# Later, larger handling of the probabilities and norms by token in a two-layer cross-attention kernel

## What is computed

```python
# layer 0: rope on q and k, a distance bias on the scores, a gated output
scores = einsum('bhqd,bhkd->bhqk', q, k) * SCALE + temporal_bias
attended = einsum('bhqk,bhkd->bhqd', softmax(scores), v) @ Wout.T + b_out
gate = sigmoid(attended @ Wgate.T + b_gate)
x = x + gate * attended + (1 - gate) * layernorm(x)
x = x + tanh(layernorm(x) @ weight @ aux_weight1 @ aux_weight2 + bias)
# layer 1: attention without a bias (the mask is all ones here), then 8 experts, 2 per token
x = x + attention(layernorm(x) @ wq.T + bq, ctx, mask) @ wo.T + bo
p = softmax(max(layernorm(x) @ gate_W + gate_b, 1e-4))
x = x + sum over the top two experts of comb * (layernorm(x) @ expert_W + expert_b) / 2
```

## Time and profile before

| | us |
|---|---|
| median of 3 runs | 582.25 |
| lowest and highest of them | 575.12, 584.12 |
| the profiled execution, device time | 577.29 |
| its span in the trace | 575.9 |
| PE, ACT, DVE, POOL busy | 514.1, 431.5, 276.9, 171.5 |

### The profile page before, as it was taken

One profiled execution on the slowest core, in us unless ns is written; L12 is line 12 of the kernel. 1 busy time (PEld: TensorE's weight loads), 2 busy tenths in 40 slices (PEclk: granted clock), 3 DMA queues, 4 the chain that ended last, 5 costly groups with the idle time before them and its releaser, 6 DMA issues.

```text
span 575.9 us, 15324 instructions
## 1 busy us (share of the span) xinstructions
PE 514.1 (89%) x6330; PEld 257.7 (45%) x6330; DVE 276.9 (48%) x715; ACT 431.5 (75%) x493; POOL 171.5 (30%) x207
## 2 busy tenths in 40 slices
PE   7688898997979998899999999999999999999993
PEld 4344445444435554455455444434443444344341
DVE  4838555864585255752521342235263435254145
ACT  1257576786678786787879988898979888988841
POOL 4467727584586316750010001000001000000003
PEclk9889999999999999999999999999999999999996
DMA  8497965399258513582364474129213911100000
GB/s 287 102 311 200 290 210 144 117 276 309 64 172 262 194 43 89 176 259 62 81 126 136 116 159 110 31 74 204 78 40 89 218 48 39 32 1 2 10 1 16
DMA packets 51584, 74.53 MB, mean 129 GB/s; under 512 B 11146, under 2 KB 40050, under 8 KB 51506
## 3 DMA queue, kind: packets, MB, share of 16 engines
q1 hardware_dynamic: 40690, 37.92, 26.4%
q0 software_dynamic: 5632, 24.07, 12.3%
q10 hardware_dynamic: 5184, 11.48, 6.3%
HBM read 39.95 MB, written 18.83 MB: 102 GB/s over the span
## 4 chain that ended last, share of the span: by engine, by line
PE 54%; ACT 16%; issue 9%; DVE 9%; POOL 6%; DMA 4%; SPq 1%; ACTq 0%; DVEq 0%; POOLq 0%
PE ps L505 21%; ACT probs L1132 14%; PE ps L481 14%; DMA q_side<-in_far_q 4%; PE ps L416 3%; PE ps L406 2%; PE ps L591 2%; DVE k_swapped L1430 2%; PE ps L410 1%; PE ps L517 1%; ACT k_parts L1159 1%; PE ps L665 1%; PE ps L541 1%; POOL k L977 1%; POOL k L979 1%
## 5 line engine op out<-in xcount | busy, mean ns | idle before, releaser
L1132 ACT ACTIVATE probs<-ps 124x1024 f32<-124x1024 f32 (+1 forms) x416 | 398.6, 1024 | 78.5 <-PE ps L486 51.2
L505 PE MATMUL ps<-probs,values 124*9 124x256 f32 (+1 forms) x3328 | 218.6, 380 | 0.1
L481 PE MATMUL ps<-q_side,k_side 64*124 64x256 bf16 (+1 forms) x1664 | 163.2, 290 | 37.2 <-ACT probs L1132 29.9
L481 PEld LDWEIGHTS ps<-q_side,k_side 64*124 64x124 bf16 (+1 forms) x1664 | 79.3, 130 | 139.9 <-ACT probs L1132 99.9
L505 PEld LDWEIGHTS ps<-probs,values 124*9 124x9 f32 (+1 forms) x3328 | 70.7, 90 | 87.0 <-issue 27.8
L1003 POOL TENSOR_TENSOR post_rstd<-post_rstd,power 128x2 f32<-128x2 f32 x12 | 8.4, 702 | 153.5 <-DVE post_rstd L1627 93.7
L949 POOL DMA_DIRECT2D mask_q<-in_mask x16 | 9.1, 570 | 131.2 <-DVE checks L1489 112.1
L486 PE MATMUL ps<-bias_near,bias_w 64*124 64x84 bf16 (+1 forms) x416 | 42.6, 200 | 0.0
L1430 DVE SCALAR_TENSOR_TENSOR k_swapped<-ps,beta_products,k_table_sb 32x496 f32<-32x496 f32 (+2 forms) x64 | 40.4, 632 | 0.9
L1499 DVE TENSOR_REDUCE sample_max<-ps 128x8 f32<-128x512 f32 x32 | 20.5, 685 | 34.9 <-PE ps L439 34.9
L416 PE MATMUL ps<-w_centred,ctx_turned 128*124 128x256 f32 (+1 forms) x104 | 31.2, 424 | 3.0 <-DVE k_swapped L1430 1.3
(11 more groups left out here) (234 smaller groups left out, 517.7 us busy)
## 6 DMA issues: line engine op xcount, KB each, us to landing
k_side<-k_scratch SPq DMA_DIRECT2D x24, 400.2 KB, 8.6
k_side<-k_parts SPq DMA_DIRECT2D x48, 124.0 KB, 2.4
k_scratch<-k_parts POOLq DMA_DIRECT2D x16, 372.0 KB, 5.2
q_side<-q_parts SPq DMA_DIRECT2D x63, 64.0 KB, 2.4
v_scratch<-values POOLq DMA_DIRECT2D x4, 936.0 KB, 10.7
values<-v_scratch SPq DMA_DIRECT2D x4, 936.0 KB, 13.8
v_scratch<-v POOLq DMA_DIRECT2D x12, 288.0 KB, 5.5
mask_q<-in_mask POOLq DMA_DIRECT2D x8, 400.5 KB, 3.4
```

What stands on the lines that cost most here:

```text
L481: last = pe.matmul(ps[0:width, bank, SQ * i:SQ * (i + 1)], kst[rows, j % 2, 2 * g + i, at], qst[rows, query_slot(j, run), 2 * g + i, :], s ...
L505: last = pe.matmul(ps[32 * i:32 * i + VC, ACC + g // 2, SQ * (g % 2):SQ * (g % 2) + SQ], v[0:rows, j % 2, t, h, :], p[0:rows, u % 4, SQ * ...
L1132: act.activation(p[0:rows, u % 4, :], ps[0:rows, s:s + 2, :].rearrange("p a n -> p (a n)"), ACT.Exp)\
```

## The change

- **From j = 3 on** (`WIDE_FROM`) the probabilities have seven buffers: the four, and three in the context's tiles, which nobody reads any more then. `values` is no longer called twice per visit but `values_at(j, pair)` times, 0 to 3, by tables; the calls of a batch add up to 52, and at most three units are behind. Where a side step runs, few values are called, in other visits three.
- **Other places for side steps.** The gate has five steps instead of nine, at slots 38, 40, 43, 45, 48 (j = 1, 2) or 8, 14, 18, 22, 26 (j = 3, 4). The experts' matmuls, two per step before, stand alone at slots 34, 38, 42, 46, and `weigh` on DVE is cut in two; samples come earlier (j = 4: 30, 34, 38; j > 4: 26, 30, 34) or later (j = 3: 34, 38, 42). Centring the experts' weights is cut in two at slots 42 and 46. `pick` comes one slot earlier. The gate's second tanh stands behind exp(slot + 3) of the third step, the experts' exponent behind exp(slot + 5).
- **Norms by token.** `post_tokens` turns x to tokens on partitions with the identity and at once multiplies the raw x with weights that `fold_weights(2)` has centred once, in j = 1; DVE takes the statistics with `bn_stats` and `bn_aggr` (`post_norm`) and multiplies the spread power into the product. The tanh reads the product from SBUF.
- **Two transfers later.** `load_token_rows(3)` stands behind exp 15 instead of 8 of j = 1; POOL's first `look_at_mask` comes after the keys of chunk 0 of j = 2's keys instead of before.
- **DVE's and SP's order.** At j = 2 `rotate_keys` stands between the two copies of the query parts. From j = 3 on one look at the mask stands ahead of the gate or experts and one ahead of `sample_maxima`. SP's `load_shift` stands ahead of `store_output`.

```diff
 def sample_at(j):
-    return (35, 37, 39) if j == 0 else (33, 35, 37) if j < NB - 1 else (34, 37, 40)
+    if j < NB - 1:
+        return (33, 35, 37) if j else (35, 37, 39)
+    return (34, 38, 42) if j == NB - 1 else (30, 34, 38) if j == NB else (26, 30, 34)
 SPREAD_X_AT = ((0, 14), (0, 17))
 QUERIES_AT = ((0, 15), (0, 18))
 TURN_RSTD_AT = {(0, 22): 1, (1, 6): 2, (2, 6): 3}
 CENTRE_X_AT = ((0, 20), (0, 34))
-FOLD_AT = ((1, 8), (1, 9))
-PICK_AT = 3
+FOLD_AT = ((1, 7), (1, 8), (1, 9))
+WIDE_FROM = NB - 1
+VALUES_AT = {NB - 1: (2, 0, 3, 3, 0, 3, 3, 0, 3, 1, 3, 0, 3, 1, 3, 3, 3, 1, 3, 1, 3, 2, 2, 2, 2, 2),
+             NB: (2, 0, 3, 3, 0, 3, 3, 0, 3, 1, 3, 0, 3, 1, 3, 2, 3, 2, 3, 2, 2, 0, 3, 1, 3, 3)}
+def values_at(j, pair):
+    if j < WIDE_FROM:
+        return 2
+    return VALUES_AT.get(j, (2, 0, 3, 3, 1, 0, 3, 3, 3, 2, 2, 1, 3, 1, 3, 1, 3, 0, 3, 1, 3, 1, 3, 1, 3, 3))[pair]
...
-    base = 38 if j < NB - 1 else 8
-    steps = (0, 2, 3, 5, 6, 8, 9, 11, 12)
-    return steps.index(slot - base) if slot - base in steps else None
-CENTRE_EXPERTS_AT = (NB, 24)
+    steps = (38, 40, 43, 45, 48) if j < NB - 1 else (8, 14, 18, 22, 26)
+    return steps.index(slot) if slot in steps else None
+CENTRE_EXPERTS_AT = ((NB, 42), (NB, 46))
...
-    steps = (8, 10, 22, 24, 26, 29)
+    steps = (8, 10, 20, 22, 34, 38, 42, 46)
...
+        def prob_slot(u):
+            return u % 4 if u < WIDE_FROM * UB else (u - WIDE_FROM * UB) % 7
+        def probs_of(u):
+            slot = prob_slot(u)
+            return p[:, slot, :] if slot < 4 else (ct[:], cn[:], tok[:].rearrange("p t d -> p (t d)"))[slot - 4][:, 0:HG * SQ]
+        def taken_ahead(u):
+            return max((w + 1 for w in range(max(u - 8, 0), u) if prob_slot(w) == prob_slot(u)), default=0)
...
+                    pe.matmul(ps[:, LOW, 0:128], centre[:], w_123[:], start=True, stop=True)
+                    pe.matmul(ps[:, LOW, 128:256], centre[:], late["L1_wq"][:], start=True, stop=True).then_inc(made[LOW], 1)
...
+            def post_tokens(b, k, weights_in, what):
+                pe.wait_ge(resid, 2 * b + 1 + k)
+                fill(LOW, "tokens", 2 * b + k)
                 for t in range(TT):
-                    last = pe.matmul(ps[:, bank, t:t + 1], psq[:, 128 * t:128 * t + 128], ones_mean[:, 0:1], start=True, stop=True)
-                last.then_inc(made[bank], 1)
+                    last = pe.matmul(ps[:, LOW, 128 * t:128 * t + 128], x[:, b * SQ + 128 * t:b * SQ + 128 * t + 128], ident[:],
+                                     start=True, stop=True)
+                last.then_inc(made[LOW], 1)
+                pe.wait_ge(folds, 3)
+                fill(HIGH, what, b)
+                pe.matmul(ps[:, HIGH, 0:SQ], weights_in, x[:, columns(b)], start=True, stop=True).then_inc(made[HIGH], 1)
...
-                elif k in (1, 5):
-                    pe.wait_ge(resid, 2 * b + 1 + (k == 5))
-                    post_mean(LOW, ("mean", 2 * b + (k == 5)), b)
-                elif k in (2, 6):
-                    post_var(HIGH, ("var", 2 * b + (k == 6)), 2 * b + (k == 6))
-                elif k in (3, 7):
-                    post_spread(LOW, ("spread", 2 * b + (k == 7)), 2 * b + (k == 7))
+                elif k == 1:
+                    post_tokens(b, 0, w_123[:], "ffn")
+                elif k == 3:
+                    post_tokens(b, 1, late["L1_wq"][:], "q1")
                 else:
-                    pe.wait_ge(seen[LOW], side.of(LOW, "spread", 2 * b + (k == 8)))
-                    fill(HIGH, "ffn" if k == 4 else "q1", b)
-                    pe.matmul(ps[:, HIGH, 0:SQ], w_123[:] if k == 4 else late["L1_wq"][:], xn[:, columns(b)], start=True, stop=True)\
-                      .then_inc(made[HIGH], 1)
-            def centre_experts():
-                pe.wait_ge(expert_in, 16 * N_EXPERT)
-                fill(LOW, "gate_w")
-                pe.matmul(ps[:, LOW, 0:E], centre[:], gw[:], start=True, stop=True).then_inc(made[LOW], 1)
-                for i, bank in enumerate((HIGH, LOW)):
-                    fill(bank, "expert_w", i)
-                    pe.matmul(ps[:, bank, :], centre[:], ew[:, 4 * i:4 * i + 4, :].rearrange("p e d -> p (e d)"), start=True, stop=True)\
-                      .then_inc(made[bank], 1)
+                    post_spread(LOW, ("spread", 2 * b + (k == 4)), 2 * b + (k == 4))
...
-                    for bank in (LOW, HIGH):
-                        fill(bank, "expert", b, k - 4)
-                    expert(b, k - 4, (LOW, HIGH))
+                    t, i = (k - 4) // 2, (5 - k) % 2
+                    bank = (LOW, HIGH)[i]
+                    fill(bank, "expert", b, t)
+                    pe.matmul(ps[:, bank, :], x[:, b * SQ + 128 * t:b * SQ + 128 * t + 128],
+                              ew[:, 4 * i:4 * i + 4, :].rearrange("p e d -> p (e d)"), start=True, stop=True).then_inc(made[bank], 1)
...
+                if j and slot == (3 if j < WIDE_FROM else 2):
...
+            taken = 0
             for u in range(0, NJ * UB, 2):
                 j, pair = u // UB, u % UB // 2
                 for w in (u + 2, u + 3):
                     if w < NJ * UB:
                         scores(w)
                 beside(j, 2 * pair)
-                for w in (u, u + 1):
-                    values(w)
+                for i in range(values_at(j, pair)):
+                    values(taken)
+                    taken += 1
...
+                load_shift(j + 1)
                 if j > NB:
                     store_output(j - NB - 1)
-                load_shift(j + 1)
...
-                if b == 2:
-                    look_at_mask(0)
                 for n in range(NC):
                     parts(b, n)
                     store_keys(b, n)
+                    if b == 2 and n == 0:
+                        look_at_mask(0)
...
-                elif k == 4:
-                    if b:
-                        act.wait_ge(q1_lo, b)
-                    act.wait_ge(made[HIGH], side.of(HIGH, "ffn", b))
-                    act.activation(ph[:], ps[:, HIGH, 0:SQ], ACT.Tanh, bias=col["b_ffn"]).then_inc(seen[HIGH], 1)
+                elif k == 2:
+                    act.wait_ge(post_normed, 2 * b + 1)
+                    act.activation(ph[:], ph[:], ACT.Tanh, bias=col["b_ffn"]).then_inc(ffn_done, 1)
...
-                elif (j, i) == (1, 8):
+                elif (j, i) == (1, 15):
...
-                if gate_at(j, i - 3) in (0, 4):
+                if gate_at(j, i - 3) in (0, 2):
                     gate(j - 1, gate_at(j, i - 3))
-                if expert_at(j, i - 7) == 1:
+                if expert_at(j, i - 5) == 1:
...
+            def post_norm(b, k, what):
+                n = 2 * b + k
+                dve.wait_ge(made[LOW], side.of(LOW, "tokens", n))
+                for t in range(TT):
+                    last = dve.bn_stats(pst[:, t, :], ps[:, LOW, 128 * t:128 * t + 128])
+                last.then_inc(seen[LOW], 1)
+                dve.wait_ge(seen[LOW], side.of(LOW, "tokens", n))
+                for t in range(TT):
+                    last = dve.bn_aggr(pmv[:, t, :], pst[:, t, :])
+                last.then_inc(post_aggr, 1)
+                dve.wait_ge(post_aggr, n + 1)
+                dve.tensor_scalar(prs[:], pmv[:, :, 1], EPS, None, ALU.add).then_inc(post_var, 1)
+                dve.wait_ge(made[HIGH], side.of(HIGH, what, b))
+                dve.tensor_copy(pg[:], ps[:, HIGH, 0:SQ]).then_inc(seen[HIGH], 1)
+                if k == 0 and b:
+                    dve.wait_ge(q1_lo, b)
+                dve.wait_ge(seen[HIGH], side.of(HIGH, what, b))
+                dve.wait_ge(made[LOW], side.of(LOW, "spread", n))
+                dve.tensor_tensor(ph[:], pg[:], ps[:, LOW, 0:SQ], ALU.mult).then_inc(seen[LOW], 1)
+                dve.wait_ge(seen[LOW], side.of(LOW, "spread", n))
+                dve.sem_inc(post_normed, 1)
...
+                post_norm(b, 0, "ffn")
+                dve.wait_ge(ffn_done, b + 1)
                 dve.tensor_tensor(x[:, cols], x[:, cols], ph[:], ALU.add).then_inc(resid, 1)
-                centre_post(LOW, 2 * b + 1, b)
-                deviate_post(HIGH, 2 * b + 1)
-                norm_post(LOW, 2 * b + 1, b)
+                post_norm(b, 1, "q1")
...
-                    query_parts(j - 2)
-                if j + 2 < NB:
+                    query_high(j - 2)
+                    rotate_keys(j + 1, 2)
+                    query_middle(j - 2)
+                    rest_of_keys(j + 1, 2)
...
+                looks = [i for part in looks_of(j) for i in part]
+                if looks:
+                    look_at_mask(looks[0])
                 if j <= NB:
                     gate(j - 1)
                     second_queries(j - 1)
                     query_parts(j - 1)
-                    if j == NB:
-                        centre_experts()
                 else:
                     project(j - NB - 1)
                     token_norm(j - NB - 1)
                     choose(j - NB - 1)
```

(19 more changed lines are left out.)

110 lines of the change are left out of this document (56 added, 54 removed).

## The result

| | before | after |
|---|---|---|
| median | 582.62 us (4 runs, 575.12 to 584.12) | 572.75 us (4 runs, 572.61 to 573.29) |
| profiled execution | 577.29 us, span 575.9 | 572.67 us, span 569.2 |

The ratio is 0.9884, 95% interval 0.9838 to 0.9931: faster by 1.2%, which is less than the 2% asked for. The forecast was 568.6 us. The medians are 9.9 us apart, the profiled executions 4.6.

What follows compares the result with a forecast made beforehand. ACT bounds from j = 3 on, PE in j = 1 and 2. Terms 4.1 - 0.6 + 1.8 + 0.8 + 0.8 + 2.2 + 1.8 + 2.8 = 13.7 us off 582.25 give 568.6 us; range 553 to 578.

Steps and rivals of the forecast that it cites:

- two later transfers: j = 1: later token rows and mask end PE's 2.66 us far-terms wait and the clock's fall behind it; gain 4.1 us.
- the shorter norms: j = 1 and 2: PE's norm falls from 2.72 to 2.12 us, twice a batch; net gain 0.9 us in each.
- within 2%: Outcome that the time changes by less than 2% (11.6 us); chance 0.44.
- the price of side steps and threes: j = 3 to 7: visits calling three values cost ACT 0.22 to about 0.6; gains 2.2 + 1.8 + 2.8.
- the copy in j = 3: `copy_sums` no longer holds the next batch's first values, as the gate's DVE chain ends sooner: 0.4 us each, together 0.8.
- The first two rivals: ACT becomes the bound, about 543 us, 0.10 (half-way 557, 0.13); visits of three cost 0.64 us each, 575 us, 0.18.
- the wait in j = 4: PE waits at `sample(5, 1)`, slot 34, for DVE's maxima behind a mask piece; 1.4 us lost.
- the bound of 0: Low bound for the two later transfers in j = 1: no gain if other traffic fills the gap; high bound 4.5 us.
- The wait of 0.72: j = 1 and 2, second to-token step at slot 45: PE waits for DVE's x, forecast as 0.8 us.
- Third fold: j = 1: the third weight fold costs PE two small matmul pairs, 0.6 us.
- DVE's order 0.8: j = 2: `rotate_keys` runs in DVE's wait for POOL, sparing PE's waits for that rotation; gain 0.8 us, bounds 0 and 3.7.

Runs made afterwards that it cites:

- the loads late in both kernels: ACT's bulk loads of j = 0 issued four exps later: on the kernel before 573.57 us, on the changed kernel 566.62 us.
- the changed kernel with the moved mask: Changed kernel, bulk loads late, to-token step and sample one slot later, POOL's mask piece ordered behind the norms' two powers: 564.81 us.
- the early loads: Kernel before with ACT's bulk loads of j = 0 issued ahead of the first exp: 582.9 us.
- the idle increments: Unused semaphore increments on VectorE: 87 on the changed kernel with the moved mask, 564.96 us; 41 on the kernel before with late loads, 576.72 us.
- the moved to-token step: Changed kernel, late loads, second to-token step (j = 1, 2) at slot 46 for 45, j = 5's second sample at 35 for 34: 565.82 us.

## Why the prediction was wrong, point by point

The forecast was a gain of 13.7 us. Measured are 1.2% (the ratio), about 7 us, and 6.95 with the loads late in both kernels. Three steps failed: two later transfers were priced from one wait at 4.1, the shorter norms at 1.8, and the start and the end of the program were put at nothing without a reason. The range (553 to 578) held the time, and "within 2%" had 0.44 beside 0.51 for "faster".

- *What bounds it, the price of side steps and threes, j = 3 to 7*: right. Forecast 2.2 + 1.8 + 2.8 = 6.8 beside 0.4 for the copy in j = 3, measured 2.4 + 2.5 + 2.2 = 7.1 with it. The first two rivals, that ACT becomes the bound and that threes cost their full 0.64, fall by the 0.58 and 0.17 above. ACT's idles are 0.25 to 0.50 in place of 1.59; the wait in j = 4 is 1.02 for 1.4.
- *Two transfers later, 4.1*: the step that failed most. Place, cause and the clock's part were right, and the pair of profiles agreed there (4.37). But the wait of 2.66 us hangs on how the start went and is 0.40 with a quiet one (the bulk loads late), and the transfers cost 0.57 where the mask's issue went and up to 1.2 at the second place near 190. The median gained 2.5 us on the kernel before as it stands and 1.3 with a quiet start. I had read the spread of 9 us between three runs as noise around a fixed program; the waits differ between executions, j = 0's above all. With a quiet start the bound of 0 that the text named for this term was nearer than the value taken.
- *Norms by token in j = 1 and 2, 1.8*: measured about 0.4 in j = 1 and -0.1 in j = 2 (the pair with late loads). In j = 2 the changed kernel loses 0.40 and 0.83 us at exps 47 and 48, behind the second to-token step, gets 1.42 back at exp 50 and loses 0.42 at the first exp of the next batch. Two shorter norms should have left more, but PE then stands 0.39 us for ACT in front of the scores at 271.18. The likely reading, argued from this row and not tested, is that in the last visits of these batches PE is no longer the bound, so that time which PE frees is lost where ACT is next. The wait of 0.72 was in the sum.
- *Third fold, -0.6*: measured -1.09 at exp 10 of j = 1 and +0.27 at exp 12, so -0.8. The third fold's own matmuls (141.33 to 141.97, 0.64 us) come behind exp 10 (139.35). What holds exp 10 is the first fold: it went one slot earlier, and its four matmuls (137.75 to 138.84) now stand in front of that exp's scores, where the kernel before had it in one visit with the second fold.
- *Copies 0.8, DVE's order 0.8*: 0.92 (0.46 twice, at exp 2 of j = 2 and 3) and 0.85 (at exp 26 of j = 2). Right.
- *The end*: not in the forecast at all. 41 more instructions on VectorE cost 1.4 us on the mean behind the last instruction.
- *The base*: the sum was made against a profiled execution 5 us below the median and then taken off the median. That carries a gain over only if the spread above the profile is the same in both kernels. It was not: in the profile after, j = 0 was 8.2 us longer by the order of two queues at the start, a term that the forecast put at nothing. That the range held the time is partly luck, since this, the missing gains and the base went opposite ways.

Worked out anew for a quiet start: 1.3 (transfers) - 0.8 (folds) + 0.3 (norms) + 0.9 (copies) + 0.85 (DVE) + 1.9 + 2.5 + 2.2 (j = 3, 4, 5 to 7) - 1.4 (end) = 7.75 us, against 6.95 measured. Both sides are uncertain by 1.6 to 1.7 us, so the sum fits, and proves little.

What sets the first exp earlier or later is not the change: the kernel before with late loads had 29.72, the changed kernel with the moved mask 31.74. Most of it is the granted clock. PE's matmuls just ahead of the first scores, in the kernel before and in the changed one:

```profile
27.17 3.66 PE L416 MATMUL ps<-w_centred,ctx_turned 128*124 128x256 f32 x8 [1.02 <-DVE v L1474]
```

```profile
26.49 1.99 PE L441 MATMUL ps<-w_centred,ctx_turned 128*124 128x256 f32 x8 [1.03 <-DVE v L1503]
```

The granted clock is 0.53 over the first stretch and 1.00 over the second, which is 1.67 of the 2.35 us. All thirteen profiles follow this: in the four with a late first exp (31.70 to 31.76, and the early loads) these eight matmuls take 3.6 to 3.7 us at 0.53 or 0.54, in the other nine 1.99 us at 1.00.

What stays open: why the clock goes one way or the other there, the remaining 0.7 us, by which the kernel before was already late at 27.17, and whether the idle increments cost anything.

## What to carry to other kernels

When runs of one program spread by more than the gain you look for, find out first which waits differ between its executions: a wait in a single trace is worth its mean over executions, not its length in that trace, and two kernels have to be compared with the loose part of the start nailed down. Bulk loads that are issued on the progress of one engine race with small urgent ones issued on that of another; tie them to what must land first. Time freed on one engine is worth only what the next wait leaves of it, as when the moved to-token step uncovered far terms that came late.

## What the runs showed of the hardware that was not expected

Blocks of instructions are loaded by DMA while the kernel runs, to the very end, and VectorE's length decides whether one or two come last. With 870 instructions 1.3 to 1.9 us lay outside the span, with 911 1.8 to 4.0, with 998 1.4 to 1.5: 87 idle instructions more made the end shorter, 41 more made it longer. That the step is every 8 KB is what the two paddings were laid out for and fits; no other length was tried. Then, a stand of PE of 2.17 us near the end of j = 1 was followed by a granted clock of 0.58 over 4 us, as the 2.66 us in the earlier trace rows was by 0.67; stands of 0.81, 1.00 and 1.97 us at the same place in three variants of the kernel before left it at 1.00.
